# Softmax exponentials of the first attention moved from PSUM to four SBUF buffers, with the score slot freed by the exponential

## The chip, the cores and the metric

The kernel runs on one core of a Trainium2 chip. The metric is the device time of one execution in microseconds (us), lower is better. TensorE is called PE here, VectorE DVE, ScalarE ACT, GpSimd POOL and SyncE SP, as in the profile.

## The reference, cut to what matters

Two transformer layers on 1024 tokens of width 256, everything in float32. The change lies in the first attention: 16 heads of width 128, full softmax over 1024 keys.

```python
qkv = (x @ w_qkv.T).reshape(B, S, 3 * H, D)
logits = jnp.einsum('bqhd,bkhd->bhqk', q, k) * scale
weights = jax.nn.softmax(logits.astype(jnp.float32), axis=-1)
combined = jnp.einsum('bhqk,bkhd->bqhd', weights, v).reshape(B, S, H * D)
return combined @ w_out.T
```

Behind it come a feed-forward block with ternary weights, a latent attention and a feed-forward block whose weights are looked up in a table of 16 values. The weights of these two feed-forward blocks are prepared while the first attention runs: the ternary weights are cut from their float32 originals, and the table lookup is done as 16 compares and adds per table.

## The kernel before, in words

**Stages.** The lists HEADS, FFN0, LATENT and FFN1 hold steps in one order for all engines; each engine walks the whole list and issues its own share of each step, in order, with waits on semaphores. HEADS is the first attention with the preparation of the later weights beside it. It takes the time from the start to about 600 us; the change touches HEADS alone.

**Units.** HEADS works in 32 units `u` (one head, one half of the 1024 queries), each with four row blocks `j` of 128 queries. For each block:

- `scores` (line 1164): PE multiplies 128 queries with 1024 keys in three float16 products (high by high, high by low, low by high), two times three matmuls by lines 1094 to 1096, into a score slot of two PSUM banks. There are three slots (`NSB = 3`, function `SB`, line 493), taken in turn.
- `max` (line 1746): DVE reads the slot and takes the row maximum.
- `exp` (lines 1502 to 1514): ACT scales the maximum (line 1511) and writes the exponential over the scores, in place in PSUM, with the row sum beside it (line 1513; the row sum is a second small instruction in the profile).
- `row_inv` (lines 1754 and 1756): DVE inverts the row sum, two small instructions.
- `cast_e` (line 1523): ACT multiplies the exponentials with the inverse and writes the float16 high half into one of three buffers of `EP`.
- `rest_e` (line 1761): DVE multiplies the exponentials again, subtracts the high half and writes the low half into `EP`. This is a scalar_tensor_tensor with a pointer scalar `rinv`, one input in PSUM (the slot) and one in SBUF (the high half).
- SP then issues a transposing DMA of both halves from `EP` to `ET16` (line 1073), and PE multiplies them with the values (`attend`, line 1202).

**When a slot is free.** Which earlier step frees a bank is worked out ahead, in lines 766 to 797. For a score slot it is `rest_e` of the block three blocks earlier (`e_lo`):

```python
                i = (4 * at[0] + at[1]) % NSB
                BANK[step] = (i, free_scores[i])
                free_scores[i] = e_lo[at]
```

**Order in a unit.** It is written out by hand (line 169): S is scores, M max, e exp, i row_inv, h cast_e, l rest_e, A attend, f and F the end of a head, X x y a projection with its two splits, O o the output projection, w weight splits, p a place for weight preparation. Blocks 0 to 2 of the next unit are worked on while unit u's last block and its attends run:

```python
    order = ("i3 f0 F0 A7 M0 S0 h3 p0 e0 l3 X0 x0 o0 i0 h0 e1 O0 y0 x1 S1 M1 l0 S2 X1 p1 w0 w1 p4 S3 i1 y1 A0 "
             "A1 X2 A2 M2 p2 l1 i2 M3 y2 h1 e2 x2 A3 A4 A5 A6 h2 l2 w2 p3 e3").split()
```

**Weight preparation beside it.** At the places p0 to p4 the steps of `prep` are dealt out. A `lut` step is one of 16 values of one table: DVE compares the index tile with the value and multiplies with the table entry into `ptm` (line 1864; line 1860 for value 0), and POOL adds `ptm` to the table (line 2101). For every fourth value POOL does the compare itself (line 2096). The two buffers of `ptm` alternate, so a compare waits for the add of two values earlier. The ternary weights are cut by DVE in pairs of instructions, lines 1844 and 1846; line 1846 is a scalar_tensor_tensor with a pointer scalar, as line 1761 is, and with both inputs in SBUF. POOL also scales and splits the attention's own weights (lines 2049, 2055, 2062, 2068, 2072, 2077).

Of the kernel before, what the change touches and what calls it, by code (L numbers as in the profile page):

```python
# [11 lines left out]
ACT = mybir.ActivationFunctionType  # L12
AX = mybir.AxisListType

P = 128
# [13 lines left out]
NE_RING = 3  # L29
# [347 lines left out]
def build(nc, a, out):  # L377
    with ExitStack() as top:
# [8 lines left out]
        def sbuf(ctx, name, shape, dt=F32):  # L387
            return ctx.enter_context(nc.sbuf_tensor(name, shape, dt))
# [3 lines left out]
        ps = top.enter_context(nc.psum_tensor("ps", [P, 8, 512], F32))  # L392
        X = sbuf(top, "X", [P, NT, D])
        XN = sbuf(top, "XN", [P, NT, D])
        XH = sbuf(top, "XH", [P, 2, 1024], F32R)
        XL = sbuf(top, "XL", [P, 2, 1024], F32R)
        ident = sbuf(top, "ident", [P, P])
# [18 lines left out]
        with ExitStack() as ctx:  # L416
# [5 lines left out]
            s_unit = sbuf(ctx, "s_unit", [P, 4])  # L422
            nms = sbuf(ctx, "nms", [P, 8])
# [8 lines left out]
            EP = sbuf(ctx, "EP", [P, NE_RING, 2, 1024], F16)  # L432
# [60 lines left out]
        def SB(u, j):  # L493
            n = (4 * u + j) % NSB
            return ps[:, 2 * n:2 * n + 2, :].rearrange("p a n -> p (a n)")
# [171 lines left out]
        for step in HEADS:  # L667
            what, at = step[0], step[1:]
# [97 lines left out]
        for step in HEADS:  # L766
            what, at = step[0], step[1:]
            if what == "turn_in":
                for k in range(2):
                    take_work((*step, k), x_lo[at[0], k, at[1]])  # L770
            elif what in ("qk", "v"):
                take_work(step, qkv_lo[step])
            elif what == "scores":
                i = (4 * at[0] + at[1]) % NSB
                BANK[step] = (i, free_scores[i])
                free_scores[i] = e_lo[at]
            elif what == "attend" and at[1] == 0:
                OB_FREE[at[0]] = free_work[1]
                attending = True
            elif what == "finish_lo":  # L780
                free_work[1] = o_lo[at]
                attending = False
                count["work"] += 1
                last_taken[1] = count["work"]
            elif what == "norm_wqk":
                take_work(step, q_norm[at])
            elif what == "norm_wv":
                take_work(step, v_norm[at])
            elif what == "turn_norm":
                take_work(step, v_unit[at])  # L790
            elif what == "out_proj":
                take_work(step, o_added[at])
            elif what == "threshold":
                take_work(step, threshold[at[0], 0])
            elif what == "up_gate":
                BANK[step] = (at[1], [free_scores[at[1]]])
                count["pair"] += 1
# [605 lines left out]
        def _(e):  # L1403
# [47 lines left out]
            for step in HEADS:  # L1451
                what, at = step[0], step[1:]
                if what == "norm_out":
                    norm_out(*at)
                elif what == "norm_in":
                    norm_in(*at)
                elif what == "turn_in":
                    turn_in(*at, WB)
                elif what == "square_wqk":
                    h, = at  # L1460
                    if h >= 2:
                        w.wait_ge(*q_normed[h - 2])
                        w.wait_ge(*q_squared[h - 2, 3])
                    for i in range(4):
                        w.wait_ge(*wqk_in[i // 2][h + i // 2])
                        if i > 0:
                            w.wait_ge(*q_squared[h, i - 1])
                        e.activation(wsq[:, :, :], wqr[:, i // 2, :, i % 2 * P:i % 2 * P + P], ACT.Square,
                                     accum_out=wsum[:, i:i + 1]).then_inc(q_squared.sem, 1)
                elif what == "split_wqk":  # L1470
                    h, = at
                    w.wait_ge(*q_scaled[h])
                    if h >= 2:
                        w.wait_ge(*projected["qk", h - 2, 0, 1])
                    e.copy(wqh[:, h % 2, :, :], wqr[:, h % 2, :, :]).then_inc(w_hi.sem, 1)
                elif what == "split_wv":
                    h, = at
                    w.wait_ge(*v_scaled[h])
                    if h >= 2:
                        w.wait_ge(*projected["v", h - 2, 3])  # L1480
                    e.copy(wvh[:, :, :], wvr[:, :, :]).then_inc(w_hi.sem, 1)
                elif what == "split_wo":
                    h, = at
                    w.wait_ge(*wo_in[h])
                    if h >= NWO:
                        w.wait_ge(*o_projected[(h - NWO) // 2, 1, 1])
                    e.copy(woh[:, h % NWO, :], wor[:, :]).then_inc(w_hi.sem, 1)
                elif what == "qk_hi":
                    h, which, half = at
                    bank, cs = ps[:, WB + BANK[("qk", *at)][0], :], slice(half * 512, half * 512 + 512)  # L1490
                    w.wait_ge(*projected[("qk", *at)])
                    if h >= 2:
                        w.wait_ge(*scored[unit_of(h - 2, (half, 1)[which]), 3])
                    e.mul((qh, kh)[which][:, h % 2, cs], bank, 1.0 / X_UP).then_inc(qkv_hi.sem, 1)
                elif what == "v_hi":
                    h, j = at
                    bank = ps[:, WB + BANK[("v", *at)][0], :].rearrange("p (i n) -> p i n", i=2)
                    w.wait_ge(*projected[("v", *at)])
                    if h >= 4:
                        w.wait_ge(*attended[2 * (h - 4) + 3, 7])  # L1500
                    e.mul(VH[:, (h // 2) % 2, 2 * j:2 * j + 2, :], bank, 1.0 / X_UP).then_inc(qkv_hi.sem, 1)
                elif what == "exp":
                    u, j = at
                    c = 4 * (u % 2) + j
                    w.wait_ge(*maxed[u, j])
                    if u >= 2:
                        w.wait_ge(*inverted[u - 2, j])
                    bank = SB(u, j)
                    h4 = unit(u)[0] % 4
                    w.wait_ge(*s_scale[unit(u)[0] // 2 * 2])  # L1510
                    e.mul(nms[:, c:c + 1], nmax[:, c:c + 1], s_unit[:, h4:h4 + 1]).then_inc(max_down.sem, 1)  # L1511
                    w.wait_ge(*max_down[u, j])
                    e.activation(bank, bank, ACT.Exp, bias=nms[:, c:c + 1], scale=s_unit[:, h4:h4 + 1],  # L1513
                                 accum_out=rsum[:, c:c + 1]).then_inc(exped.sem, 1)
                elif what == "cast_e":
                    u, j = at
                    n = 4 * u + j
                    c = 4 * (u % 2) + j
                    w.wait_ge(*inverted[u, j])
                    if n >= NE_RING:  # L1520
                        old = ((n - NE_RING) // 4, (n - NE_RING) % 4)
                        w.wait_ge(*e_turned[n % NE_RING][old])
                    e.mul(EP[:, n % NE_RING, 0, :], SB(u, j),  # L1523
                          rinv[:, c:c + 1]).then_inc(e_hi.sem, 1)
                elif what == "finish_hi":
                    u, = at
                    w.wait_ge(*attended[u, 7])
                    h, half = unit(u)
                    if u >= 4:
                        w.wait_ge(*o_projected[u // 4 - 1, half, 1])  # L1530
                    w.wait_ge(*v_unit[h - h % 2])
                    e.mul(OH[:, u % 4, :], OB, vinv[:, h // 2 % 2, h % 2:h % 2 + 1]).then_inc(o_hi.sem, 1)
                elif what == "abs_sum":
                    m, c = at
                    w.wait_ge(*raw_in[m])
                    e.activation(tern[:, m, c * 512:c * 512 + 512], raw[:, c * 512:c * 512 + 512], ACT.Abs,
                                 accum_out=tsum[:, 4 * m + c:4 * m + c + 1]).then_inc(abs_summed.sem, 1)
                elif what == "silu_table":
                    silu_table()
                elif what == "reuse":  # L1540
                    w.each(POINT["heads"].values())
# [111 lines left out]
        def _(e):  # L1653
# [59 lines left out]
            for step in HEADS:  # L1713
# [43 lines left out]
                elif what == "rest_e":  # L1757
                    u, j = at
                    c, n = 4 * (u % 2) + j, 4 * u + j
                    w.wait_ge(*e_hi[u, j])  # L1760
                    e.scalar_tensor_tensor(out=EP[:, n % NE_RING, 1, :], in0=SB(u, j),  # L1761
                                           scalar=rinv[:, c:c + 1], in1=EP[:, n % NE_RING, 0, :], op0=ALU.mult,
                                           op1=ALU.subtract).then_inc(e_lo.sem, 1)
                elif what == "out_add":
# [498 lines left out]
```

## Time and profile before

| what | us |
|---|---|
| median of 3 runs (lowest 938.06, highest 946.85) | 938.49 |
| time of the profiled execution | 939.58 |
| its span, first to last instruction | 937.8 |
| mean granted PE clock, share of full speed | 0.985 |
| busy: PE, DVE, ACT, POOL | 827.9, 775.4, 646.5, 427.3 |

The span is the time from the first to the last instruction of the profiled execution; the 1.8 us by which its time is longer lie around it. "Busy" is the sum of the durations of an engine's instructions. A wait is put down to the instruction whose semaphore came last. Matmuls overlap one another, so a busy PE is not one at its peak.

### The profile page before, as it was taken

The numbers are of one execution on the slowest core, as the hardware profiler recorded it, in microseconds if no ns is written. First come the engines' busy times: TensorE is split into PE (matmuls) and PEld (weight loads), VectorE is DVE, ScalarE is ACT, GpSimd is POOL, SyncE is SP. The second block draws the span as 40 slices with busy tenths as digits, with TensorE's granted clock in tenths as the row PEclk, the third lists the DMA queues.
The fourth block names the chain that finished last, engine by engine and source line by source line (L and its number), as shares of the span: only waits on it lengthen the run. The fifth ranks groups of instructions, "written<-read, shape, count | busy, mean of one in ns | idle before, by whom it ended". The sixth has DMA issues, their size and how long they took to land.

```text
span 937.8 us, 13391 instructions
## 1 busy us (share of the span) xinstructions
PE 827.9 (88%) x4330; PEld 471.9 (50%) x4330; DVE 775.4 (83%) x1605; ACT 646.5 (69%) x1170; POOL 427.3 (46%) x439
## 2 busy tenths in 40 slices
PE   2799989999999989988989998589878999998997
PEld 1344444454455454454445454367655555554686
DVE  2689999899989999999999998575689686885637
ACT  3588868887888777777877878454555757667631
POOL 3124354444454357777778673161322434443301
PEclk9999999999999999999999999799989999999999
DMA  3288757967778677776865677330000000000001
GB/s 121 35 160 191 154 97 156 193 115 146 174 142 153 131 136 143 149 128 135 161 124 108 127 137 142 60 104 1 1 1 1 1 0 2 0 2 1 1 1 45
DMA packets 276870, 86.32 MB, mean 92 GB/s; under 512 B 267584, under 2 KB 272448, under 8 KB 276416
## 3 DMA queue, kind: packets, MB, share of 16 engines
q1 hardware_dynamic: 275520, 80.05, 44.5%
q0 software_dynamic: 992, 5.34, 1.8%
q8 instruction: 34, 0.56, 0.2%
q14 instruction: 36, 0.29, 0.1%
q10 hardware_dynamic: 288, 0.07, 0.0%
HBM read 17.29 MB, written 1.05 MB: 20 GB/s over the span
## 4 chain that ended last, share of the span: by engine, by line
DVE 39%; PE 30%; issue 14%; ACT 12%; DMA 3%; POOL 2%; SPq 1%; POOLq 0%; ACTq 0%; DVEq 0%
DVE nmax L1746 9%; DVE EP L1761 8%; DVE ptm L1864 4%; PE ps L1094 4%; PE ps L1117 4%; PE ps L1096 4%; PE ps L1095 4%; PE ps L1355 3%; PE ps L1341 3%; PE ps L1132 3%; PE ps L1320 3%; DVE ps L1950 2%; ACT ps L1513 2%; DVE ql L1728 2%; DVE st L1661 1%
## 5 line engine op out<-in xcount | busy, mean ns | idle before, releaser
L1523 ACT ACTIVATE EP<-ps,rinv 128x1024 f16<-128x1024 f32 x128 | 142.6, 1114 | 42.0 <-DVE rinv L1756 41.5
L1761 DVE SCALAR_TENSOR_TENSOR EP<-ps,rinv,EP 128x1024 f16<-128x1024 f32 x128 | 163.2, 1276 | 5.3 <-ACT EP L1523 5.1
L1746 DVE TENSOR_REDUCE nmax<-ps 128x1 f32<-128x1024 f32 x128 | 155.7, 1217 | 0.6 <-PE ps L1096 0.6
L1513 ACT ACTIVATE ps<-ps,nms,s_unit 128x1024 f32<-128x1024 f32 x128 | 150.7, 1177 | 4.3
L1094 PE MATMUL ps<-kh,qh 128*128 128x512 f16 x256 | 98.3, 384 | 26.6 <-DVE EP L1761 24.5
L2101 POOL TENSOR_TENSOR wgu<-wgu,ptm 128x688 f32<-128x688 f32 x60 | 100.4, 1673 | 42.4 <-DVE ptm L1864 40.4
L1094 PE MATMUL ps<-ET,VH 128*128 128x512 f16 x256 | 98.3, 384 | 16.2 <-DMA ET<-EP 9.6
L1095 PE MATMUL ps<-ET,VH 128*128 128x512 f16 x256 | 98.3, 384 | 0.0
L1096 PE MATMUL ps<-ET,VL 128*128 128x512 f16 x256 | 98.0, 383 | 0.0
L1095 PE MATMUL ps<-kl,qh 128*128 128x512 f16 x256 | 97.5, 381 | 0.0
L1096 PE MATMUL ps<-kh,ql 128*128 128x512 f16 x256 | 97.5, 381 | 0.0
L2101 POOL TENSOR_TENSOR wdn<-wdn,ptm 128x512 f32<-128x512 f32 x45 | 57.7, 1282 | 80.0 <-DVE ptm L1864 78.8
L1617 ACT ACTIVATE ET<-ps 128x512 f32<-128x512 f32 (+3 forms) x144 | 62.9, 497 | 37.3 <-PE ps L1341 36.5
L1950 DVE CUSTOM_DVE_ANT_0 ps<-ps,tern 128x512 f32<-128x512 f32 (+3 forms) x128 | 71.9, 603 | 15.4 <-PE ps L1320 15.2
L1511 ACT ACTIVATE nms<-nmax,s_unit 128x1 f32<-128x1 f32 x128 | 37.6, 294 | 57.6 <-DVE nmax L1746 57.2
L2016 POOL TENSOR_TENSOR rs<-ve,mhalf 128x4 f32<-128x4 f32 (+2 forms) x22 | 19.8, 898 | 122.4 <-DVE ve L1666 98.2
L1094 PEld LDWEIGHTS ps<-kh,qh 128*128 128x128 f16 x256 | 24.9, 97 | 66.9 <-DVE EP L1761 41.4
L2163 POOL TENSOR_SCALAR_AFFINE_SELECT ET<-ET 128x128 f32<-128x128 f32 x96 | 28.1, 292 | 65.0 <-ACT ET L1617 58.3
L1094 PE MATMUL ps<-xh,wqh 128*128 128x512 f16 x128 | 49.4, 386 | 4.8 <-POOL wql L2055 4.0
L1094 PEld LDWEIGHTS ps<-ET,VH 128*128 128x128 f16 x256 | 26.0, 101 | 49.3 <-DMA ET<-EP 12.1
L1095 PE MATMUL ps<-xl,wqh 128*128 128x512 f16 x128 | 49.0, 383 | 0.0
L1096 PE MATMUL ps<-xh,wql 128*128 128x512 f16 x128 | 49.0, 383 | 0.0
(251 smaller groups left out, 2132.5 us busy)
## 6 DMA issues: line engine op xcount, KB each, us to landing
wqr<-in_wqk SPq DMA_DIRECT2D x16, 256.0 KB, 3.7
wgu<-in_tern POOLq DMA_DIRECT2D x3, 1024.0 KB, 6.3
wvr<-in_wv SPq DMA_DIRECT2D x8, 256.0 KB, 4.2
wor<-in_wo SPq DMA_DIRECT2D x16, 128.0 KB, 3.4
ET<-EP SPq DMA_TRANSPOSE x128, 4.3
X<-in_x SPq DMA_DIRECT2D x2, 512.0 KB, 5.7
prw<-in_down_idx POOLq DMA_DIRECT2D x2, 256.0 KB, 6.4
tern<-in_l_wuq_rep SPq DMA_DIRECT2D x1, 512.0 KB, 4.9
```

The source lines that it names most:

```text
L1094: e.matmul(dst, lh, rh, start=first, stop=False)
L1095: e.matmul(dst, lh, rl, start=False, stop=False)
L1096: return e.matmul(dst, ll, rh, start=False, stop=last)
L1117: mm = e.matmul(ps[:, 2 * r + o, :], l, m, start=i == 0, stop=i == len(pairs) - 1)
L1511: e.mul(nms[:, c:c + 1], nmax[:, c:c + 1], s_unit[:, h4:h4 + 1]).then_inc(max_down.sem, 1)
L1513: e.activation(bank, bank, ACT.Exp, bias=nms[:, c:c + 1], scale=s_unit[:, h4:h4 + 1], accum_out=rsum[:, c:c + 1]).then_inc(exped.sem, 1)
L1523: e.mul(EP[:, n % NE_RING, 0, :], SB(u, j), rinv[:, c:c + 1]).then_inc(e_hi.sem, 1)
L1617: e.activation(ET[:, r, c:c + n1], ps[:, BANK[(*step, c)][0], n - n1:n], ACT.Exp).then_inc(weight_exped.sem, 1)
L1746: e.tensor_reduce(nmax[:, c:c + 1], SB(u, j), AX.X, ALU.max, negate=True).then_inc(maxed.sem, 1)
L1761: e.scalar_tensor_tensor(out=EP[:, n % NE_RING, 1, :], in0=SB(u, j), scalar=rinv[:, c:c + 1], in1=EP[:, n % NE_RING, 0, :], op0=ALU.mult, ...
L1950: e.tensor_tensor_reduce(src, src, mask[:, m0:m0 + n], 1.0, -3.0e38 if part == 0 else half, ALU.add, ALU.max, NM[:, p % 2, i8, col:col + 1 ...
L2101: e.tensor_tensor(dst, dst, ptm[:, v % 2, 0:n], ALU.add).then_inc(lut_added.sem, 1)
```

## The change

The exponential is written to a new float32 tile `E32` in SBUF, with one buffer of 1024 columns for each of the four blocks `j`. `cast_e` (ACT) and `rest_e` (DVE) read it there in place of the slot. A score slot is free behind `exp` of three blocks earlier (`exped`), no longer behind `rest_e`. As buffer `j` is used again by the next unit, `exp` waits for `rest_e` of the same block of the unit before. `E32` is allocated in a scope that is closed at once, so that its 16 KB per partition are given again to the tiles after it, `XH` and `XL`, which are first written when the first attention's scores are done.

```diff
         XN = sbuf(top, "XN", [P, NT, D])
+
+        with ExitStack() as ctx:
+            E32 = sbuf(ctx, "E32", [P, 4, 1024])
...
                 BANK[step] = (i, free_scores[i])
-                free_scores[i] = e_lo[at]
+                free_scores[i] = exped[at]
...
                     w.wait_ge(*max_down[u, j])
-                    e.activation(bank, bank, ACT.Exp, bias=nms[:, c:c + 1], scale=s_unit[:, h4:h4 + 1],
+                    if u >= 1:
+                        w.wait_ge(*e_lo[u - 1, j])
+                    e.activation(E32[:, j, :], bank, ACT.Exp, bias=nms[:, c:c + 1], scale=s_unit[:, h4:h4 + 1],
                                  accum_out=rsum[:, c:c + 1]).then_inc(exped.sem, 1)
...
-                    e.mul(EP[:, n % NE_RING, 0, :], SB(u, j),
+                    e.mul(EP[:, n % NE_RING, 0, :], E32[:, j, :],
                           rinv[:, c:c + 1]).then_inc(e_hi.sem, 1)
...
-                    e.scalar_tensor_tensor(out=EP[:, n % NE_RING, 1, :], in0=SB(u, j),
+                    e.scalar_tensor_tensor(out=EP[:, n % NE_RING, 1, :], in0=E32[:, j, :],
                                            scalar=rinv[:, c:c + 1], in1=EP[:, n % NE_RING, 0, :], op0=ALU.mult,
                                            op1=ALU.subtract).then_inc(e_lo.sem, 1)
```

## Rows read from the trace of the kernel before

**Rows 1.** The page: busy time of each engine, and engines of the last chain.
```profile
PE 827.9 (88%) x4330; PEld 471.9 (50%) x4330; DVE 775.4 (83%) x1605; ACT 646.5 (69%) x1170; POOL 427.3 (46%) x439
...
DVE 39%; PE 30%; issue 14%; ACT 12%; DMA 3%; POOL 2%; SPq 1%; POOLq 0%; ACTq 0%; DVEq 0%
```

**Rows 2.** Two stretches: us, busy PE, PEld, DVE, ACT, POOL, clock, DMA share, GB/s.
```profile
60.00:340.00 280.00, 261.50 (x1364) 136.16 (x1362) 260.53 (x439) 224.72 (x395) 119.94 (x96) 0.99 0.77 149
340.00:570.00 230.00, 211.78 (x1104) 108.50 (x1103) 223.19 (x343) 177.36 (x293) 172.89 (x107) 1.00 0.72 134
```

**Rows 3.** Groups of the page: busy us, mean ns, idle before, who ended it.
```profile
L1523 ACT ACTIVATE EP<-ps,rinv 128x1024 f16<-128x1024 f32 x128 | 142.6, 1114 | 42.0 <-DVE rinv L1756 41.5
L1761 DVE SCALAR_TENSOR_TENSOR EP<-ps,rinv,EP 128x1024 f16<-128x1024 f32 x128 | 163.2, 1276 | 5.3 <-ACT EP L1523 5.1
L1746 DVE TENSOR_REDUCE nmax<-ps 128x1 f32<-128x1024 f32 x128 | 155.7, 1217 | 0.6 <-PE ps L1096 0.6
L1513 ACT ACTIVATE ps<-ps,nms,s_unit 128x1024 f32<-128x1024 f32 x128 | 150.7, 1177 | 4.3
L1094 PE MATMUL ps<-kh,qh 128*128 128x512 f16 x256 | 98.3, 384 | 26.6 <-DVE EP L1761 24.5
```

**Rows 4.** What DVE waited for, 60 to 340 us: total us, times, longest.
```profile
DVE rsc L1754 <- ACT ps L1513: 3.7, 11, 0.5
...
DVE OL L1824 <- ACT OH L1532: 3.4, 10, 0.5
DVE wnorm L1780 <- PE ps L1183: 1.9, 4, 0.5
```

**Rows 5.** Two lines of DVE and one of POOL by source: duration ns min/median/max.
```profile
L1846 DVE SCALAR_TENSOR_TENSOR tern<-wgu,tsc,tern x12: 750/752/1646, 125.2 to 330.9; 128x512 bf16<-128x512 f32 x12
...
L1824 DVE SCALAR_TENSOR_TENSOR OL<-ps,vinv,OH x32: 731/750/752, 66.7 to 608.7; 128x512 fp32r<-128x512 f32 x32
...
L2101 POOL TENSOR_TENSOR wdn<-wdn,ptm x45: 1260/1270/1450, 76.4 to 342.3; 128x512 f32<-128x512 f32 x45
```

**Rows 6.** Timeline, DVE and POOL meeting: start, duration, instruction.
```profile
232.47 1.65 DVE L1846 SCALAR_TENSOR_TENSOR tern<-wgu,tsc,tern 128x512 bf16<-128x512 f32 x1
...
232.12 1.45 POOL L2101 TENSOR_TENSOR wdn<-wdn,ptm 128x512 f32<-128x512 f32 x1 [6.50 <-DVE ptm L1864]
...
483.55 0.75 DVE L1864 TENSOR_SCALAR ptm<-wgu,lut 128x688 f32<-128x688 int32 x1
...
483.09 2.58 POOL L2096 TENSOR_SCALAR ptm<-wgu,lut 128x688 f32<-128x688 int32 x1
```

**Rows 7.** Timeline of DVE and POOL over one unit, 432 to 450 us.
```profile
432.51 1.27 DVE L1761 SCALAR_TENSOR_TENSOR EP<-ps,rinv,EP 128x1024 f16<-128x1024 f32 x1
...
435.69 1.28 DVE L1761 SCALAR_TENSOR_TENSOR EP<-ps,rinv,EP 128x1024 f16<-128x1024 f32 x1
...
432.67 1.63 POOL L2101 TENSOR_TENSOR wgu<-wgu,ptm 128x688 f32<-128x688 f32 x1 [0.46 <-DVE ptm L1864]
435.56 0.73 POOL L2077 TENSOR_TENSOR wol<-wor,woh 128x256 fp32r<-128x256 f32 x1 [1.26 <-ACT woh L1487]
...
447.12 1.15 POOL L2055 TENSOR_TENSOR wql<-wqr,wqh 128x512 f16<-128x512 f32 x1
448.24 3.69 POOL L2101 TENSOR_TENSOR wgu<-wgu,ptm 128x688 f32<-128x688 f32 x2
...
448.57 1.27 DVE L1761 SCALAR_TENSOR_TENSOR EP<-ps,rinv,EP 128x1024 f16<-128x1024 f32 x1
```

**Rows 8.** The same stretch by line: first POOL's line 2096, then DVE's 1864.
```profile
340.00:570.00 230.00, 43.34 (x17) 1.00 0.72 134
...
340.00:570.00 230.00, 40.11 (x44) 1.00 0.72 134
```

**Rows 9.** Groups of ACT, HEADS: source in SBUF, then in PSUM, mean ns.
```profile
L1475 ACT CAST wqh<-wqr 128x512 f16<-128x512 f32 x16 | 9.8, 616 | 2.6 <-POOL wqr L2049 2.6
...
L1494 ACT ACTIVATE kh<-ps 128x512 f16<-128x512 f32 x32 | 18.8, 587 | 6.9 <-PE ps L1096 6.9
```

## Prediction

> **What bounds the kernel now.** I read the page first, then busy time by stretch, the costliest groups, the waits of DVE and PE, and last the timelines of DVE and POOL. The page's chain shows 39% of the span on DVE and 30% on PE [rows 1]. The change touches the first attention only, so its stage decides. I cut its steady part in two: 60 to 340 us, where POOL is lightly loaded, and 340 to 570 us, where nearly all table lookups of width 688 run. DVE is busy 260.5 of 280 us (93%) in the first and 223.2 of 230 us (97%) in the second; PE 93% and 92%; ACT 80% and 77% [rows 2]. So DVE bounds the second stretch, and DVE and PE together the first.
>
> Of the steps touched, the reader should see four groups. PE stood idle 24.5 us before scores because `rest_e` (line 1761) had not freed the slot. But the maximum (line 1746), the first reader of those scores on DVE, waited 0.6 us for PE in all its 128 times [rows 3]. The wait that the change removes is PE's, and PE's lateness hardly reaches DVE by that door. What DVE does wait for: 3.7 us for the row sums of ACT, 3.4 us for the end of a head on ACT (which waits for attends), 1.9 us for small matmuls [rows 4].
>
> **The change part by part.**
>
> *The slot free behind the exponential.* It removes up to 24.5 us of PE idle time. With DVE full, only DVE's own idle time can be won: 280 - 260.5 = 19.5 us and 230 - 223.2 = 6.8 us [rows 2], together 26, the upper end of this gain. Most of it PE does not cause. What PE feeds are the two later of these waits, 5.3 us [rows 4]; with some start-up effect I take 6 us as won. Lower end: 0.
>
> *The length of `rest_e` alone.* Its first input moves from PSUM to SBUF. No such instruction of 1024 columns is in the trace. The nearest pair of 512 columns, both with pointer scalar and a second input in SBUF, is 752 ns with the first input in SBUF (line 1846) and 750 ns with it in PSUM (line 1824) [rows 5]. So 1276 ns stays, within 2 x 2 ns x 128 = 0.5 us: 0. The Trainium skill, "VectorE: DVE Perf Modes", section on the TRN2 errata, gives 58 fixed cycles for SBUF and 120 for PSUM sources, by which each would be 65 ns shorter and the sum, as an estimate, 8 us less. The measured pair shows no such difference, so the sum has none of it.
>
> *`rest_e` beside POOL.* Now both its inputs lie in SBUF, as in line 1846 only. That line takes 0.75 us at the least and the median [rows 5]. At 232.47 it took 1.65 us: POOL's add (line 2101) had run since 232.12 and ended at 233.57, 1.10 us after line 1846 began, and line 1846 was 0.90 us longer. It waited out the add but for about 0.20 us [rows 6]. Its longest is 1646 ns [rows 5]. Line 1761 never varies: with its first input in PSUM it does not meet POOL. After the change its 128 instructions would. The opposite holds too: that add, the longest of 45 with 1.45 us against a median of 1.27 [rows 5], had itself been held by DVE's line 1844, which still ran when it began. Not every instruction of POOL counts: a compare of line 1864 that began within POOL's line 2096, of 2.58 us, took 0.75 us [rows 6] and not the 2.7 us of a full wait, so I price line 2096 at 0.2 us a meeting.
>
> The Trainium skill, "SBUF — State Buffer", section "Who interferes with whom", says that a DVE instruction with two SBUF inputs and a GpSimd instruction that reads SBUF exclude each other for their whole length. The trace agrees for line 2101 (0.90 of 1.10 us) and not for line 2096 (about 0.2 of 2.1 us); by the rule alone the rival "POOL blocks fully" below would be the forecast.
>
> Now count. I laid the 128 starts of line 1761 on POOL's timeline. Lower bound, nothing else moving: 12 starts of 60 to 340 us fall in POOL instructions other than line 2096, with 7.5 us of them left; 16 of 340 to 570 us with 6.7 us (one is 435.69, in line 2077 of 435.56 to 436.29 [rows 7]); one at the end with 1.6 us. Less 0.2 each: 5.1 + 3.5 + 1.4 = 10 us. 20 more fall in line 2096: 20 x 0.2 = 4. Floor 14 us.
>
> But POOL moves too. In 340 to 570 us, 30 of its instructions begin within a `rest_e` and would be pushed to its end, by 27.9 us together; 432.67 is one, behind 432.51, pushed by 1.1 us. Pushed adds end later and meet the next `rest_e` or compare. One unit by hand [rows 7]: the `rest_e` at 435.69 waits 0.4 us for line 2077; at 448.57 two adds stand queued behind line 2055 (447.12), and if the first gets in ahead, that `rest_e` waits 1.63 - 0.20 = 1.4 us; the other three of the five lose up to 0.2 us together. That is 0.6 to 2.0 us in five, middle 1.3, 0.26 each, and 53 x 0.26 = 14 us. The compares (line 1864, 44 taking 40.1 us [rows 8]) are blocked today already, 0.57 us being their length alone; with later adds I give each 0.1 us, 4 us. In 60 to 340 us I double the floor for the pushes, 10 us, and let DVE's slack take a third: 7 us. With the 1.4 us at the end: 14 + 4 + 7 + 1 = 26 us.
>
> Upper end: in 340 to 570 us POOL without line 2096 is 172.9 - 43.3 = 130 us, `rest_e` 53 x 1.276 = 68, compares 44 x 0.57 = 25: 223 of 230 us that would exclude one another [rows 2, 8]. If such a load only packs to 85%, the stretch is 262 us, 32 us longer; with 10 us of the first stretch, and a DVE that then waits for late adds (the two `ptm` buffers), some 50.
>
> *ACT.* `cast_e` reads SBUF: 616 against 587 ns [rows 9], +0.03 us. The exponential writes SBUF: between 1114 ns (line 1523, PSUM to SBUF) and 1177 ns as now plus the same 0.03; I take no change. 128 x 0.03 = 4 us of ACT lie under DVE (ACT is 77 to 80% busy). Where DVE waits for the row sum anyway nothing changes, as the exponential keeps its length. A later `cast_e` can delay `rest_e`, which waited 5.1 us for it in all [rows 3]: six times 0.03 is under 1 us. I count 0; bounds -1 and +2.
>
> *The new wait.* `exp` of block j waits for `rest_e` of block j one unit before. Queued behind it on ACT are `cast_e` and the projection's splits, and DVE's `row_inv` needs it. But `exp` also waits for its own maximum, which DVE issues, in its order, behind that `rest_e`; so it is fulfilled when reached: 0. No DMA is added; the transposes go with `rest_e` and come later only as it does.
>
> **Sum.** +26 - 6 = +20 us on the profiled execution: span 937.8 to 958, time 939.58 to 959.6. That execution is 1.1 us above the median, so from 938.49 the forecast is 958 us.
>
> **The rivals.** About 1% is what a measurement of this kernel tells from no change: 929.1 to 947.9 us.
>
> 1. *It stays at the floor.* For it: POOL's adds begin mostly right behind a compare, which stands just before a `rest_e` in the order, so they slip behind it and end in the 2.7 us before the next (four intervals from 432.51 to 448.57 [rows 7], 16.06 / 4, less 1.28). Against it: 223 of 230 us leave little room to slip. Cost 14, of which slack takes 2, gain 6: +6, 944 us, within 1%.
> 2. *POOL blocks fully, or the lookups become the bound.* Line 2096 then holds `rest_e` for its whole rest (20 meetings, 24.5 us left in them, so +20), or adds fall so far behind that DVE's compares wait. Against it: the 0.75 us of line 1864 [rows 6]. 938.5 + 45 = 984 us.
> 3. *Faster: early scores let DVE close its gaps.* One mechanism, PE running ahead in the score slots so that attends, head ends and splits come earlier; its place is DVE's 26 us of idle time. For it: PE's 24.5 us. It decides once the blocking costs less than what is won: with blocking at 8 us (POOL slipping behind `rest_e` nearly always) and half the idle time, 13, won, it is -5, 933 us; at no blocking and 19 us won, 919. Against it: DVE waits 0.6 us for scores.
> 4. *It does nothing:* the slot is freed early, DVE is full either way and the meetings fall into slack: 938 us.
>
> **How the numbers follow.** Forecast 958 (947.9 to 972): 0.52. Full blocking, 984: 0.16. Floor, 944: 0.14. Nothing: 0.07. Faster, 933 down to 919: 0.11, of which 0.07 is by over 1%. Slower by over 1%: 0.52 + 0.16 = 0.68, and 0.02 of the floor's, 0.70; within 1%: the rest, 0.23. The range for 8 in 10 goes from 932 us (part of the faster case) to 986.
>
> **What would show it.** Right: line 1761 no longer even but from 1.27 to about 2.7 us, mean near 1.45, longer only where POOL's adds or splits run; line 2101 with a longer mean and starts behind `rest_e`; PE's wait for line 1761 gone and its idle time moved to attends and splits; the stretches of lookups growing most; nothing moved after 600 us but the start. Wrong: line 1761 even at 1.276 us, or DVE's share falling while the stage gets shorter.

## The result, and the profile after

The median went from 938.83 us (four runs) to 961.16 us (four, 960.23 to 961.72): a ratio of 1.022, with the interval from 1.016 to 1.027. The forecast was 958 us, slower by over 1%. The profiled execution took 961.04 us and its span 959.3 us, 21.5 more than the span before.

The page of the kernel after: first busy time of each engine, then the engines of the last chain, then groups (busy us, mean ns, idle before, who ended it). They answer to [rows 1, 3].

```profile
PE 831.9 (87%) x4330; PEld 471.2 (49%) x4330; DVE 793.0 (83%) x1605; ACT 650.7 (68%) x1170; POOL 474.6 (49%) x439
...
DVE 43%; PE 25%; issue 15%; ACT 11%; DMA 4%; POOL 2%; SPq 0%; POOLq 0%; DVEq 0%; ACTq 0%
...
L1766 DVE SCALAR_TENSOR_TENSOR EP<-E,rinv,EP 128x1024 f16<-128x1024 f32 x128 | 180.9, 1414 | 6.7 <-ACT EP L1528 6.2
L1518 ACT ACTIVATE E<-ps,nms,s_unit 128x1024 f32<-128x1024 f32 x128 | 154.2, 1205 | 4.3
L1528 ACT ACTIVATE EP<-E,rinv 128x1024 f16<-128x1024 f32 x128 | 146.9, 1148 | 57.0 <-DVE rinv L1761 56.2
L2106 POOL TENSOR_TENSOR wgu<-wgu,ptm 128x688 f32<-128x688 f32 x60 | 122.0, 2033 | 35.3 <-DVE ptm L1869 32.6
L2106 POOL TENSOR_TENSOR wdn<-wdn,ptm 128x512 f32<-128x512 f32 x45 | 71.5, 1589 | 78.1 <-DVE ptm L1869 77.0
L1097 PE MATMUL ps<-kh,qh 128*128 128x512 f16 x256 | 98.1, 383 | 5.0 <-DVE kl L1733 4.9
```

The lines have moved by some: `rest_e` is 1766 (before 1761), `cast_e` 1528, the exponential 1518, the maximum 1751, DVE's compare 1869, POOL's add 2106, POOL's own compare 2101. With the same instruction counts, DVE is 17.6 us busier, as much as `rest_e` grew (163.2 to 180.9 us), and POOL 47.3 us. POOL's adds grew from 1673 to 2033 ns and from 1282 to 1589. PE no longer waits for `rest_e` before scores; it did so for 24.5 us [rows 3]. DVE's share of the chain rose from 39 to 43%.

One line by source: duration ns min/median/max, first and last start. The first fence is of the kernel before, the second of after.

```profile
L1761 DVE SCALAR_TENSOR_TENSOR EP<-ps,rinv,EP x128: 1270/1275/1285, 38.7 to 591.9; 128x1024 f16<-128x1024 f32 x128
```

```profile
L1766 DVE SCALAR_TENSOR_TENSOR EP<-E,rinv,EP x128: 1272/1277/2684, 38.6 to 611.9; 128x1024 f16<-128x1024 f32 x128
...
L2106 POOL TENSOR_TENSOR wgu<-wgu,ptm x60: 1635/1910/2659, 360.8 to 587.5; 128x688 f32<-128x688 f32 x60
```

The least and the median of `rest_e` did not move, its longest went from 1285 to 2684 ns, and its last start is 20.0 us later. So moving the input does not change the instruction; meeting others does. I laid its 128 instructions on POOL's timeline. 30 are longer than alone, by 17.6 us together: 12 met adds (11.1 us), 9 met line 2082, the split of the output weights (2.9), 7 met POOL's own compare (2.7), 2 met line 2067 (0.9). By block `j` the losses are 0.1, 9.5, 4.3 and 3.6 us for blocks 0 to 3: in the written order block 1's `rest_e` (l1) stands right behind a compare (p2), so an add is due just when it begins.

The timeline of the kernel after shows three of these meetings, one that went the other way, and one that cost nothing (start, duration, instruction; "idle before" in brackets). First DVE, then POOL.

```profile
434.94 1.92 DVE L1869 TENSOR_SCALAR ptm<-prw,lut 128x688 f32<-128x688 int32 x1
436.77 1.28 DVE L1766 SCALAR_TENSOR_TENSOR EP<-E,rinv,EP 128x1024 f16<-128x1024 f32 x1
...
440.54 1.28 DVE L1766 SCALAR_TENSOR_TENSOR EP<-E,rinv,EP 128x1024 f16<-128x1024 f32 x1
...
445.51 2.66 DVE L1766 SCALAR_TENSOR_TENSOR EP<-E,rinv,EP 128x1024 f16<-128x1024 f32 x1
450.08 1.70 DVE L1766 SCALAR_TENSOR_TENSOR EP<-E,rinv,EP 128x1024 f16<-128x1024 f32 x1
454.23 1.79 DVE L1766 SCALAR_TENSOR_TENSOR EP<-E,rinv,EP 128x1024 f16<-128x1024 f32 x1
```

```profile
436.93 2.61 POOL L2106 TENSOR_TENSOR wgu<-wgu,ptm 128x688 f32<-128x688 f32 x1 [0.45 <-DVE ptm L1869]
439.64 2.58 POOL L2101 TENSOR_SCALAR ptm<-prw,lut 128x688 f32<-128x688 int32 x1
...
445.16 4.51 POOL L2106 TENSOR_TENSOR wgu<-wgu,ptm 128x688 f32<-128x688 f32 x2
449.98 0.72 POOL L2082 TENSOR_TENSOR wol<-wor,woh 128x256 fp32r<-128x256 f32 x1 [0.31 <-ACT woh L1490]
454.11 2.59 POOL L2101 TENSOR_SCALAR ptm<-prw,lut 128x688 f32<-128x688 int32 x1
```

At 436.77 `rest_e` began 0.16 us ahead of the add and kept its 1.28 us; the add took 2.61 instead of some 1.64, 0.97 of the 1.12 that `rest_e` still had. At 445.51 the add was 0.35 us ahead: `rest_e` took 2.66, 1.38 longer, of the 1.58 that the add still ran, and the second of the two queued adds then waited in its turn (4.51 us for both). At 450.08 a split had 0.62 us left and cost 0.42. At 454.23 POOL's own compare had 2.47 us left and cost only 0.51; at 440.54 another had 1.68 left and cost nothing. In this trace it depends on how far the compare has got: 24 `rest_e` began within one; the 7 that did so in its first 0.43 us took 0.21 to 0.51 us longer, and the 17 that began 0.51 us or more behind its start took no longer. For the 7, the compare's start and the end of the extra time are 0.63 to 0.72 us apart.

PE's and DVE's waits after, 60 to 600 us (total us, times, longest). The same list of before begins for PE with 22.6 us for `rest_e`, and DVE's with 7.4 for the row sum, 4.3 for the head's end (OL), 3.5 for `cast_e` and 3.3 for wnorm.

```profile
PE ps L1097 <- DMA ET<-EP: 15.5, 18, 4.2
PE ps L1097 <- DVE VL L1743: 13.5, 15, 2.9
PE ps L1097 <- DVE ql L1733: 7.6, 9, 1.3
PE ps L1097 <- DVE OL L1829: 6.8, 10, 1.4
PE ps L1097 <- DVE kl L1733: 6.6, 6, 1.6
...
DVE rsc L1759 <- ACT E L1518: 6.2, 15, 0.5
DVE EP L1766 <- ACT EP L1528: 4.6, 7, 1.0
DVE OL L1829 <- ACT OH L1537: 3.6, 7, 1.0
DVE wnorm L1785 <- PE ps L1186: 3.3, 7, 0.5
```

PE's wait moved to the transposes and to DVE's splits. DVE's own idle time hardly shrank: the four waits are 18.5 us before and 17.7 after, where a single new one of 2.4 us (VL for ACT) stands beside them. Nearly nothing of what PE won reached DVE.

**The start.** A part of the loss comes before any table of width 688. The stretches 74 to 78 and 78 to 82 us (busy PE, PEld, DVE, ACT, POOL, granted clock, DMA share, GB/s), first of before, then of after with PE's first wait of 45 to 92 us.

```profile
74.00:78.00 4.00, 3.48 (x21) 1.84 (x20) 3.97 (x8) 3.60 (x7) 2.37 (x2) 1.00 0.94 182
78.00:82.00 4.00, 4.00 (x22) 2.00 (x21) 3.97 (x6) 3.33 (x7) 2.35 (x3) 1.00 0.45 86
```

```profile
74.00:78.00 4.00, 0.30 (x2) 0.00 (x0) 3.96 (x8) 3.63 (x7) 2.10 (x2) 1.00 0.83 143
78.00:82.00 4.00, 3.52 (x13) 1.84 (x14) 3.11 (x5) 0.81 (x2) 2.50 (x2) 0.62 0.72 153
...
PE ps L1097 <- DMA ET<-EP: 4.2, 1, 4.2
```

PE, with its scores done early, reaches the attends, waits 4.2 us for one transpose, and the granted clock of the next stretch is 0.62 of full speed (1.00 before), part of it at the lower of the two levels. It then does in those 4 us 13 matmuls instead of 22, and ACT is 0.81 us busy instead of 3.33. In the chain the transpose is 7.85 us long, from 70.38 to 78.23:

```profile
70.38 7.85 DMA ET<-EP
```

The 13th `rest_e` starts at 89.1 us before and 93.4 after, of which 0.4 us is longer `rest_e`: about 4 us are lost here.

**The account of the span.** Up to the last start of `rest_e`, DVE's busy time: `rest_e` +17.7; DVE's compares together -1.7 (57.9 to 56.2 us, 77 of them); its other lines +1.9. DVE's idle time: +3.8 up to the 13th `rest_e`, -1.7 behind it. That is 20.0, as the last start of `rest_e` says. Behind it +1.1: the last `rest_e` now holds POOL's small line 2021 (2016 before), 1.04 to 2.08 us, and DVE's wait for the line that needs it rose from 0.8 to 1.9. Together 21.1 of 21.5. These are two single executions; the executions of one kernel lie up to some us apart, so the smaller terms are less sure than the large ones.

### The profile page after: what moved, and what is told of

It is laid out like the page before. It is cut to its first block, busy times and chain, and to the rows that moved or that the text cites. A ratio compares the mean times of both kernels' runs of the same rounds, so it can differ in the third digit from the quotient of the medians.

```text
span 959.3 us, 13515 instructions
## 1 busy us (share of the span) xinstructions
PE 831.9 (87%) x4330; PEld 471.2 (49%) x4330; DVE 793.0 (83%) x1605; ACT 650.7 (68%) x1170; POOL 474.6 (49%) x439
## 4 chain that ended last, share of the span: by engine, by line
DVE 43%; PE 25%; issue 15%; ACT 11%; DMA 4%; POOL 2%; SPq 0%; POOLq 0%; DVEq 0%; ACTq 0%
DVE nmax L1751 11%; DVE EP L1766 11%; PE ps L1120 4%; DVE ptm L1869 4%; PE ps L1358 3%; DVE ps L1955 3%; PE ps L1135 3%; PE ps L1344 3%; PE ps L1097 2%; DMA ET<-EP 2%; PE ps L1099 2%; PE ps L1098 2%; PE ps L1323 2%; ACT E L1518 2%; DVE ql L1733 2%
## 5 line engine op out<-in xcount | busy, mean ns | idle before, releaser
L1766 DVE SCALAR_TENSOR_TENSOR EP<-E,rinv,EP 128x1024 f16<-128x1024 f32 x128 | 180.9, 1414 | 6.7 <-ACT EP L1528 6.2
L1528 ACT ACTIVATE EP<-E,rinv 128x1024 f16<-128x1024 f32 x128 | 146.9, 1148 | 57.0 <-DVE rinv L1761 56.2
L1518 ACT ACTIVATE E<-ps,nms,s_unit 128x1024 f32<-128x1024 f32 x128 | 154.2, 1205 | 4.3
L2106 POOL TENSOR_TENSOR wgu<-wgu,ptm 128x688 f32<-128x688 f32 x60 | 122.0, 2033 | 35.3 <-DVE ptm L1869 32.6
L2106 POOL TENSOR_TENSOR wdn<-wdn,ptm 128x512 f32<-128x512 f32 x45 | 71.5, 1589 | 78.1 <-DVE ptm L1869 77.0
L1955 DVE CUSTOM_DVE_ANT_0 ps<-ps,tern 128x512 f32<-128x512 f32 (+3 forms) x128 | 71.8, 603 | 14.9 <-PE ps L1323 14.8
L1097 PE MATMUL ps<-wvh,xh 128*128 128x256 f16 x128 | 36.3, 283 | 16.3 <-DVE VL L1743 6.3
```

Source lines behind the costliest of these rows:

```text
L1097: e.matmul(dst, lh, rh, start=first, stop=False)
L1518: e.activation(E32[:, j, :], bank, ACT.Exp, bias=nms[:, c:c + 1], scale=s_unit[:, h4:h4 + 1], accum_out=rsum[:, c:c + 1]).then_inc(exped.s ...
L1528: e.mul(EP[:, n % NE_RING, 0, :], E32[:, j, :], rinv[:, c:c + 1]).then_inc(e_hi.sem, 1)
L1766: e.scalar_tensor_tensor(out=EP[:, n % NE_RING, 1, :], in0=E32[:, j, :], scalar=rinv[:, c:c + 1], in1=EP[:, n % NE_RING, 0, :], op0=ALU.mu ...
L1955: e.tensor_tensor_reduce(src, src, mask[:, m0:m0 + n], 1.0, -3.0e38 if part == 0 else half, ALU.add, ALU.max, NM[:, p % 2, i8, col:col + 1 ...
L2106: e.tensor_tensor(dst, dst, ptm[:, v % 2, 0:n], ALU.add).then_inc(lut_added.sem, 1)
```

## The experiments

**The slot freed as before.** The exponentials stay in SBUF; a score slot is free behind `rest_e` again.

```diff
-                free_scores[i] = exped[at]
+                free_scores[i] = e_lo[at]
```

> The changed kernel with one part undone: a score slot is again free only behind rest_e; the exponentials stay in SBUF. Theory (the port): the 128 rest_e still meet POOL, so they are longer by 14 to 20 us together (17.7 in the changed kernel), and PE, which again waits for rest_e before scores (over 15 us), no longer runs ahead at 60 to 80 us; its single wait of 4.2 us for the transposing DMA and the fall of the clock behind it are gone. 955 to 960 us. Rival 1 (the early slot gives several us back): slower than the changed kernel, 964 us or more. Rival 2 (PE running ahead is the loss, not the port): 942 us or less.

958.92 us, a ratio of 1.020 (1.017 to 1.022) to before. `rest_e` is 2.4 us longer in all than with the early slot (20.1 over before, where 14 to 20 were expected), and PE's wait for it is back, longer than before. `rest_e` alone in the stretch to 640 us (busy us, times, clock, DMA share, GB/s), and PE's first wait of 45 to 600 us:

```profile
0.00:640.00 640.00, 183.32 (x128) 0.98 0.67 131
...
PE ps L1097 <- DVE EP L1766: 29.7, 36, 2.3
```

So 29.7 us of PE's waiting, given back, cost no time: the early slot wins nothing in the whole. The slowdown belongs to the buffers in SBUF. `rest_e` is 20.1 us longer and the compares 1.4 shorter than before: 18.7, beside a time of 18.4. That the two lie so close is in part chance: in the trace the last `rest_e` starts 16.9 us later, as DVE's idle time up to there fell by 3.1 and its other lines grew by 1.3, and 2.8 us come behind it.

**POOL's adds without their reads**, in both kernels. Each add to a table becomes a write of a constant over the same columns, so the lookups' sums are left out; POOL's instruction is 701 instead of 1673 ns long at width 688, and reads nothing.

```diff
-                        e.tensor_tensor(dst, dst, ptm[:, v % 2, 0:n], ALU.add).then_inc(lut_added.sem, 1)
+                        e.memset(dst, 0.01).then_inc(lut_added.sem, 1)
```

The kernel after:

> The changed kernel with POOL's 105 adds of the table lookup (12 of the 30 meetings, 11.1 of the 17.6 us) replaced by a write of a constant to the same tile, which reads nothing from SBUF; order, waits and DVE's compares are kept, the lookups themselves are left out. Theory (the port): no rest_e is longer beside these writes; what is left is the splits and POOL's compares, 4 to 8 us of lengthening. The kernel comes within 8 to 13 us of the same edit to the kernel before. Rival (the length comes from SBUF reads as such or from ACT's longer exponential and cast): the distance between the two stays near 22 us.

The kernel before:

> The control: the kernel before with the same edit, the 105 adds replaced by writes of a constant (the lookups are left out). Theory: rest_e stays at 1276 ns as it never met POOL; compares (line 1864), which the adds lengthened by about 17 us in all, become shorter, as far as writes do not lengthen them: 922 to 936 us. Rival (compares are not on the path): 938 us.

935.92 and 926.23 us, ratios to the kernel before of 0.996 (0.994 to 0.998) and 0.986 (0.982 to 0.989). The change costs 9.7 us here, 22.3 with the adds. `rest_e` and then the compares, to 640 us, of the kernel after with the writes:

```profile
0.00:640.00 640.00, 167.78 (x128) 0.97 0.68 133
...
0.00:640.00 640.00, 44.64 (x77) 0.97 0.68 133
```

Of the 17.7 us 13.1 are gone. 4.6 remain; the splits and POOL's own compares had made 6.5 of it with the adds. So the adds are the larger share. The writes are shorter than the adds as well, so fewer meetings might do it too; the trace decides for the reads: 48 `rest_e` run beside a write, 7 of them begin within one, and none takes over 1.286 us. Of the 9.7 us, 4.6 are `rest_e` and 1.0 the compares; most of the rest lies in DVE's idle time, 2.5 us of it up to the 13th `rest_e`, where PE waited 3.6 us for one transpose. The control shows a second thing: the kernel before pays for them too. Its compares are 57.88 us busy with the adds and 43.65 without, 14.2 less, and the time is 14.3 less than before's 940.5 in the same job. That loss the change did not bring; it was there.

**The loads moved past the start**, in both. The first five lookups of width 512 go to the front, so that the first ternary load, of 1 MB, is issued at 84.78 us in the kernel after and no longer at 68.61, just before the long transpose.

```diff
-    prep = []
+    prep, width = width[:5], width[5:]
```

> The changed kernel with one size moved: the first load of 1 MB of ternary weights is dealt out behind five lookup steps, one unit later. Theory: the loss of 4 us between 68 and 89 us comes from one transposing DMA that took 7.9 us beside this load (5.8 before) while PE, having run ahead, had nothing else; with the load elsewhere PE's longest wait for a transposing DMA falls below 2.5 us and the kernel gains 2 to 5 us, 956 to 959 us. Rival (the wait is PE's running ahead alone, whatever the load): no change, 960 to 962 us.

> Control to the changed kernel with the later load: the kernel before with the first load of ternary weights behind five lookup steps. PE does not run ahead here and waited 0.5 us for that transposing DMA; so no time is to be won at the start, and only the meetings of compares and adds change: within 2 us of the kernel before. If it moves by more, the result of the later load in the changed kernel cannot be read as the start-up wait alone.

960.14 and 946.62 us, ratios of 1.021 (1.019 to 1.024) and 1.006 (1.003 to 1.008). PE's wait of 45 to 95 us for a transpose fell from 4.2 to

```profile
PE ps L1097 <- DMA ET<-EP: 2.3, 1, 2.3
```

as expected, but the time did not follow, and the control lost some 6 us by itself, where nothing was expected. The traces show where: the loss at the start moved with the load. In the changed kernel the 13th `rest_e` now starts at 89.0 us (89.1 before), and the loss comes after it. In the control, which has no early slot, the load is in flight from 83.62 to 92.33 us. The transpose beside it is as long as the one in the changed kernel was, PE waits for it, and the clock of the next stretch is low. The control's transpose in its chain, PE's wait of 66 to 110 us, and two stretches as above:

```profile
86.08 8.12 DMA ET<-EP
...
PE ps L1094 <- DMA ET<-EP: 2.8, 1, 2.8
...
90.00:94.00 4.00, 1.59 (x7) 0.51 (x6) 3.97 (x8) 3.60 (x7) 3.40 (x3) 1.00 0.97 195
94.00:98.00 4.00, 3.55 (x10) 1.36 (x11) 1.57 (x4) 0.58 (x2) 3.62 (x3) 0.57 1.26 146
```

Between the 14th and the 15th `rest_e` the control takes 7.6 us, the kernel before 3.6. So the long transposes go with the load: the longest beside the first two loads took 7.85 and 8.01 us in the kernel after, 8.12 and 8.18 in the control, and 5.77 and 7.75 in the kernel before, where 4.3 is the median. Not every long one is waited for: around the 7.75 us of the kernel before, PE never stood idle for as long as 1.5 us. The loss at the start is therefore one of the early slot and the load's place together, and the kernel before pays a like one when the load is elsewhere. The change costs 13.5 us between these two. How the load makes the transpose longer is not shown.

**The compares behind `rest_e`**, in both. If the place right behind a compare is what makes blocks 1 and 3 pay, turning two pairs of the order round should help.

```diff
-    order = ("i3 f0 F0 A7 M0 S0 h3 p0 e0 l3 X0 x0 o0 i0 h0 e1 O0 y0 x1 S1 M1 l0 S2 X1 p1 w0 w1 p4 S3 i1 y1 A0 "
-             "A1 X2 A2 M2 p2 l1 i2 M3 y2 h1 e2 x2 A3 A4 A5 A6 h2 l2 w2 p3 e3").split()
+    order = ("i3 f0 F0 A7 M0 S0 h3 e0 l3 p0 X0 x0 o0 i0 h0 e1 O0 y0 x1 S1 M1 l0 S2 X1 p1 w0 w1 p4 S3 i1 y1 A0 "
+             "A1 X2 A2 M2 l1 p2 i2 M3 y2 h1 e2 x2 A3 A4 A5 A6 h2 l2 w2 p3 e3").split()
```

> The changed kernel with two places of weight preparation moved in the hand-written order: p0 from in front of l3 to behind it, p2 from in front of l1 to behind it. Of the 17.6 us by which rest_e grew, 9.5 us fell on block 1, whose rest_e stands right behind the compare of p2, with the adds of p1 and p4 still running or queued. Theory (the port, and who is queued when): an add then starts behind rest_e and ends beside the row maximum, and the compare, 1.3 us later, finds the earlier adds done. rest_e grows by 4 to 9 us in all, not 17.6, the compares are shorter too, and the kernel takes 945 to 953 us. Rival (a meeting avoided at one place comes back at the next, as the port is nearly full): no gain, 958 us or more.

> The kernel before with the same two places moved. rest_e has one input in PSUM and meets nothing; only the compares can win, which the adds lengthen by 17 us, 12 of them at p0 and p2 behind the row maximum. Theory: the compares that stand behind a rest_e meet less (5.3 us in 30 there against 11.9 in 32 here): 932 to 937 us, ratio 0.993 to 0.998. Rival (the compares' waits just move): 938 to 940 us.

After with this order: 966.03 us, 1.027 (1.024 to 1.029). Before with it: 933.69 us, 0.992 (0.990 to 0.995). `rest_e` of the first, then the compares of the second, to 640 us:

```profile
0.00:640.00 640.00, 190.39 (x128) 0.98 0.66 129
```

```profile
0.00:640.00 640.00, 49.55 (x77) 0.98 0.67 133
```

In the kernel after the expectation missed and its rival came: `rest_e` lengthens by 27.2 us instead of 17.7, in 50 meetings instead of 30. Block 1 (l1) hardly gained, 9.0 instead of 9.5 us; it meets adds for 4.2 and POOL's split of line 2060 for 2.7. Blocks 2 and 3 lose 8.0 and 10.0 instead of 4.3 and 3.6, of which 3.9 and 7.8 beside adds. In the kernel before, where `rest_e` does not meet POOL, the compares get 8.3 us shorter, and the time 7.0 us. One order of work is good for one kernel and bad for the other. This version, at 0.992, beats both kernels.

**Every compare in front of a `rest_e`**, in both: the reverse, so that `rest_e` begins ahead of the add that the compare releases. The two lines take the place of the same two as above.

```diff
+    order = ("i3 f0 F0 A7 M0 S0 h3 p0 p4 e0 l3 X0 x0 o0 i0 h0 e1 O0 y0 x1 S1 M1 p1 l0 S2 X1 w0 w1 S3 i1 y1 A0 "
+             "A1 X2 A2 M2 p2 l1 i2 M3 y2 h1 e2 x2 A3 A4 A5 A6 h2 p3 l2 w2 e3").split()
```

> The changed kernel with every place of weight preparation put in front of a rest_e: p0 and p4 before l3, p1 before l0, p2 before l1, p3 before l2. The moved order before this one put them behind and made it worse (rest_e longer by 26.9 us in all, not 17.6): an add then runs until the next rest_e. Theory (who comes first at the port): a rest_e right behind a compare goes ahead of that compare's add, which has 2.2 to 2.9 us until the next compare. rest_e grows by 3 to 10 us, the compares by less than 12, and the kernel takes 944 to 953 us. Rival (the port is too full for any order): 958 us or more.

> The same order in the kernel before. rest_e meets nothing there; only the compares, 16.9 us longer in all in the kernel before and 8.7 with the two places moved behind rest_e, can change. Theory: what counts for them is the distance from one compare to the next; four of five are now a block apart: 6 to 10 us, 931 to 936 us. Rival (only places behind rest_e help): 938 us or more.

966.66 and 953.83 us, 1.029 (1.028 to 1.030) and 1.015 (1.013 to 1.017). Both missed. The control fell although its compares came out almost alone, and its waits of 45 to 600 us point at the reason:

```profile
0.00:640.00 640.00, 43.36 (x77) 0.98 0.68 133
...
PE ps L1094 <- DVE EP L1761: 35.2, 35, 2.8
...
DVE OL L1824 <- ACT OH L1532: 14.8, 22, 1.1
DVE rsc L1754 <- ACT ps L1513: 10.0, 27, 0.8
DVE EP L1761 <- ACT EP L1523: 8.0, 6, 3.7
```

Two compares in front of l3 and one in front of each other put `rest_e` off; PE waits longer for its slot, the head ends later, and DVE itself idles (4.3 us for OL before, 14.8 here). Here PE's wait for slots went with idle time of DVE. It fits that the change costs only 12.8 us in this order (966.66 less 953.83), although `rest_e` lengthens by 19 and the compares by 4.4: the early slot would give something back where slots are late. I did not try that by itself.

**The early slot from unit 3 on.** The release stays `rest_e` for units 0 to 2 and is the exponential from unit 3.

```diff
-                free_scores[i] = exped[at]
+                free_scores[i] = exped[at] if at[0] >= 3 else e_lo[at]
```

> The changed kernel with the old release (behind rest_e) for the slots of units 0 to 2 and the new one from unit 3 on. Theory: the early slot costs about 4 us once, at 70 to 90 us, where PE runs out of work and its clock falls, and gives nothing later, as DVE is full; so this kernel is as the one with the old release throughout, 956 to 960 us. Rival (the early slot gives back some us in the steady part, hidden by the loss at the start): 955 us or less.

956.65 us, 1.017 (1.016 to 1.019). `rest_e` to 640 us, and the two stretches of the start:

```profile
0.00:640.00 640.00, 180.30 (x128) 0.99 0.67 133
...
74.00:78.00 4.00, 2.42 (x11) 1.02 (x12) 3.97 (x8) 3.63 (x7) 1.35 (x2) 1.00 1.08 215
78.00:82.00 4.00, 4.00 (x26) 2.36 (x25) 3.97 (x6) 3.33 (x6) 3.26 (x2) 1.00 0.32 62
```

The hole in PE and the lower clock are gone, and the 13th `rest_e` starts at 91.0 us, 1.9 later than before, of which 1.4 is lengthening: 0.5 us remain, not 4. `rest_e` +17.1 and compares -0.4 make 16.7, beside 16.6 of time. As in the first experiment that is in part chance: the last `rest_e` starts 14.5 us later. Against the change as it was this is 4.5 us by the medians; but the intervals of the two ratios overlap, so what shows the loss at the start are the rows of the trace, and its size is less sure than its place. Against the first experiment, old release throughout, it is nothing: 1.017 and 1.020, intervals that overlap. Where the order is the written one, the early slot gives nothing later on either.

## Why the prediction was right

The time, the sign and the mechanism came as forecast. That the time came so close is in part luck, as two terms were off and made up for each other: the meetings, DVE's compares counted in, cost 16.0 us where 26 were forecast, nearer to the 14 of the rival "floor", and the slot lost about 4 where 6 were to be won.

- *The slot, 6 us won, 0 to 26 as bounds:* wrong, and outside its bounds. The step that failed is "with some start-up effect I take 6 us as won" with its lower end 0. PE's 24.5 us did go, but DVE's four waits shrank by only 0.8, and the start-up effect was a loss of 4 us. The early slot lets PE run to the next thing it waits for, here a transpose beside a load; one wait of 4.2 us at the attends, with the low clock behind it, was worse than several short ones at the scores. That was to be seen in no row, but a bound below zero should have stood there.
- *`rest_e` alone, 0:* right, 1277 against 1275 ns at the median. The 65 ns less that the Trainium skill ("VectorE: DVE Perf Modes", section on the TRN2 errata) would give are not here.
- *`rest_e` beside POOL, 14 + 7 + 1 = 22 us:* right in kind and place, somewhat too much: 17.7. Up to 331 us it was 5.3 (7 forecast), behind that 12.3 (15). One count in it was a little low: from 60 to 340 us 15 starts fall in POOL's instructions other than line 2096, with 9.0 us left, not 12 with 7.5. It is 30 meetings of 0.59 us on the mean, where I had spread 0.26 over each instruction of the later stretch.
- *POOL's own compare at 0.2 us a meeting, 20 meetings:* 24 began within it, but only 7 paid, 0.21 to 0.51 us each: 2.7 us against 4. A price for each meeting was the wrong form; what counts is the first 0.63 to 0.72 us of the compare. The Trainium skill, "SBUF — State Buffer", section "Who interferes with whom", by which it would exclude `rest_e` for its whole length, does not agree: 2.47 us were left at 454.23 and 0.51 was paid. For the adds it nearly does: 1.38 of 1.58 us paid at 445.51.
- *DVE's compares, +4 us:* wrong in sign, -1.7. Pushed adds do not only move into the next compare; some move out of one, behind `rest_e`; this was not followed add by add.
- *ACT, 0 on the path:* right, with one price missed. The cast grew by 34 ns as taken from [rows 9]; the exponential, which I left at 1177, by 28. That is 8 us of ACT and not 4. It was 80 and 77% busy, and DVE's wait for the row sum did not grow; its wait for the cast grew by 1.1.
- *The new wait, 0:* right. No wait of the exponential for `rest_e` is in ACT's list of 60 to 600 us.
- *Nothing moved after 600 us but the start:* right but for 1.1 us. The last `rest_e` holds POOL; I had looked at the meeting from DVE's side only.

The first experiment and the pair with the writes carry the mechanism: with the old release the loss stays, without the adds' reads it falls by more than half, and no `rest_e` is longer beside a write. The rival "faster" falls, since giving the 29.7 us of waiting back to PE cost nothing; "full blocking" falls by the meetings with POOL's compare; "the floor" came close in the meetings, with 14, but expected 6 us of the slot.

## What to carry to other kernels

Before moving a DVE operand from PSUM to SBUF, count the SBUF inputs that remain: an instruction that did not meet GpSimd's (1270 to 1285 ns here) may become one that does (up to 2684), and the price is not the instruction but its meetings, which can be estimated from the two timelines. An earlier release is worth at most the idle time of the engine that bounds the stage, not that of the engine that waits; here PE waited 24.5 us less and DVE's four waits shrank by 0.8. And look for meetings that the kernel already pays: in the kernel before, compares held by adds were worth 7 us of time for a change of two places in the order.

## What the runs showed of the hardware that I had not expected

- Who begins first goes first, in both directions: an add 0.16 us behind `rest_e` waited 0.97 us, a `rest_e` 0.35 us behind an add waited 1.38. Even a POOL instruction on 4 columns beside the last `rest_e` took 2.08 us, 1.04 before.
- POOL's own compare, of 2.0 to 2.6 us and with one SBUF input, held `rest_e` only near its own start: 0.21 to 0.51 us in the 7 that began in its first 0.43 us, nothing in the 17 that began 0.51 us or later. A write of POOL, which reads nothing, held none of 48.
- The exponential into SBUF is 28 ns longer than in place in PSUM (1205 against 1177 ns at 1024 columns), the cast out of SBUF 34 ns longer than out of PSUM (1148 against 1114).
- One wait of 4.2 us on PE was followed by a stretch at a granted clock of 0.62; in the run that freed the slot early only from unit 3 on, and in the kernel before, that wait is not there (0.4 and 0.5 us) and the stretch has 1.00. With the load moved, a wait of 2.8 us in the control was followed by 0.57, one of 2.3 us in the changed kernel by 1.00.
- A transpose takes 4.3 us at the median. The longest beside each 1 MB load took 7.75 to 8.18 us for five of the twelve loads in four traces (before, after, and both with the load moved), and 5.1 to 7.3 for the other seven.
